# Folding a root-mean-square norm into the layer norm ahead of it, in a four-stage transformer kernel

## The reference, cut to what matters

```python
def _layernorm(x, axis=-1, eps=1e-05):
    m = mean(x); v = var(x)
    return (x - m) / sqrt(v + eps)

x = x + _L1_ffn_ref(_layernorm(x), ...)

def _L1_ffn_ref(hidden_states, norm_weight, router_w, ...):
    var = mean(square(hidden_states))                  # over the 128 features
    normed = hidden_states * rsqrt(var + 1e-08) * norm_weight
    probs = sigmoid(normed @ router_w.T)               # 8 experts, the best 2 are kept
    ...                                                # shared expert and 8 experts on normed
```

## Time and profile before

| | before |
|---|---|
| median of three runs | 5244.87 us |
| the profiled execution: its own time | 5246.2 us |
| the profiled execution: span of the trace | 5244.2 us |
| TensorE busy | 5028.0 us, 96% |
| VectorE busy | 3879.9 us, 74% |
| ScalarE busy | 3424.6 us, 65% |
| GpSimd busy | 2705.6 us, 52% |
| mean granted TensorE clock | 0.97 |

### The profile page before, as it was taken

The page is one execution under the profiler, slowest core; times in us unless marked ns, Lnnn a source line. Parts: engine busy times, 40 slices in busy tenths (PEclk is TensorE's granted clock), DMA queues, the critical chain, the costliest instruction groups (busy, mean ns, idle before and its releaser), DMA issues.

```text
span 5244.2 us, 175418 instructions
## 1 busy us (share of the span) xinstructions
PE 5028.0 (96%) x76384; PEld 3279.3 (63%) x76384; DVE 3879.9 (74%) x5095; ACT 3424.6 (65%) x5293; POOL 2705.6 (52%) x1425
## 2 busy tenths in 40 slices
PE   8899999999999999999999999986999999989999
PEld 5577777677777777777777777763333333266767
DVE  5888888888888888888888888846777677533333
ACT  2588888788888888888888877742666556621111
POOL 2877777777777777777777777731111111110000
PEclk8999999999999999999999999986999999979999
DMA  2011111111111111111111111103111111000000
GB/s 74 25 40 46 31 34 39 47 35 30 38 48 35 34 31 49 37 35 31 47 42 31 34 39 42 33 22 85 20 20 20 20 20 20 2 37 4 4 4 4
DMA packets 98013, 168.24 MB, mean 32 GB/s; under 512 B 25081, under 2 KB 36866, under 8 KB 96898
## 3 DMA queue, kind: packets, MB, share of 16 engines
q1 hardware_dynamic: 94402, 147.99, 10.4%
q10 hardware_dynamic: 2880, 9.44, 1.2%
HBM read 47.37 MB, written 10.49 MB: 11 GB/s over the span
## 4 chain that ended last, share of the span: by engine, by line
PE 32%; DVE 29%; issue 20%; ACT 16%; POOL 1%; SPq 1%; DMA 1%; ACTq 0%; DVEq 0%; POOLq 0%
DVE TOK L966 8%; DVE ss L857 8%; PE D L1414 5%; PE D L1436 5%; PE D L1123 5%; PE D L1517 5%; ACT L636 4%; DVE rs L906 4%; DVE mx L927 4%; PE D L1394 4%; ACT hh L636 4%; ACT kTb L623 3%; ACT kTb L627 1%; PE D L251 1%; DVE hh L947 1%
## 5 line engine op out<-in xcount | busy, mean ns | idle before, releaser
L473 POOL TENSOR_TENSOR rn<-ss,mhalf 128x33 f32<-128x33 f32 (+2 forms) x198 | 1095.7, 5534 | 332.9 <-DVE ss L859 315.7
L998 DVE TENSOR_REDUCE mxp<-D 128x2 f32<-128x1024 f32 (+3 forms) x640 | 675.6, 1064 | 239.6 <-PE D L1394 129.3
L477 POOL TENSOR_TENSOR hh<-hh,rr 128x1024 f32<-128x1024 f32 x192 | 365.4, 1903 | 469.2 <-DVE rr L911 469.2
L746 ACT ACTIVATE V<-D 128x1024 f32<-128x1024 f32 (+3 forms) x426 | 381.8, 897 | 245.3 <-PE D L1414 243.3
L966 DVE TENSOR_TENSOR TOK<-D,wA 128x1024 f32<-128x1024 f32 x384 | 466.5, 1215 | 0.0
L857 DVE TENSOR_REDUCE ss<-TOK 128x32 f32<-128x2048 f32 x192 | 437.1, 2276 | 0.0
L1330 PE MATMUL D<-PTb,V 64*64 64x32 f32 x24576 | 405.6, 220 | 6.0 <-issue 4.9
L1330 PEld LDWEIGHTS D<-PTb,V 64*64 64x64 f32 x24576 | 381.7, 135 | 32.0 <-issue 8.1
L906 DVE TENSOR_REDUCE rs<-hh 128x16 f32<-128x1024 f32 x192 | 234.2, 1220 | 205.9 <-ACT hh L636 205.9
L664 ACT ACTIVATE V<-D 128x512 f32<-128x512 f32 x384 | 229.7, 598 | 237.8 <-PE D L1298 173.0
L481 POOL TENSOR_TENSOR XC<-XC,TOK 128x1024 f32<-128x1024 f32 x128 | 303.1, 2368 | 47.7 <-DVE TOK L966 47.7
(11 more groups left out here) (240 smaller groups left out, 11877.1 us busy)
## 6 DMA issues: line engine op xcount, KB each, us to landing
V<-V SPq DMA_DIRECT2D x936, 64.0 KB, 2.0
V<-V SPq DMA_DIRECT2D x192, 192.0 KB, 2.5
RB<-watt_dram SPq DMA_DIRECT2D x12, 512.0 KB, 3.9
X<-watt_dram SPq DMA_DIRECT2D x12, 512.0 KB, 3.8
parts_dram<-hh SPq DMA_DIRECT2D x48, 128.0 KB, 2.4
TOK<-parts_dram ACTq DMA_DIRECT2D x36, 128.0 KB
RA<-parts_dram SPq DMA_DIRECT2D x12, 384.0 KB
X<-parts_dram SPq DMA_DIRECT2D x12, 384.0 KB
```

The costliest lines, as they stand in the source:

```text
L473: pool.tensor_tensor(rn[:, st % 2, lo:hi], ss[:, st % 2, lo:hi], mhalf[:, lo:hi], ALU.pow).then_inc(s["powed"], 1)
L477: pool.tensor_tensor(sh, sh, rr[:, :].unsqueeze(2).to_broadcast([P, HEADS, 64]), ALU.mult).then_inc(s["pnorm"], 1)
L746: act.activation(PTE[i % 3][:, 2 * hp:2 * hp + 2, 0:CH - r * P], pair_of(("S", i + LAG, hp))[:, :].rearrange("p (h n) -> p h n", h=2)[:, : ...
L998: dve.tensor_reduce(mxp[:, 2 * hp:2 * hp + 2, qt, kc], pair_of(("F", at, hp))[:, :].rearrange("p (h n) -> p h n", h=2)[:, :, 0:keys], AX.X ...
```

## The change

The second norm is no longer computed. The constant added to the mean square of the first norm becomes a multiplication and an addition, v * (1 + 1e-8) + 1e-5 * 1e-8, so that the power -0.5 of it is the factor of both norms. The applying instruction of this norm becomes a `scalar_tensor_tensor`, which multiplies the centred chunk by the norm's weight and by the spread factor and writes XS directly; so ScalarE's eight scalings go too. The load of `mvec` moves from the transfers of the experts' weights to ahead of the load of `wC`, with a semaphore of its own, `mvec_in`, for which VectorE waits ahead of the norm; `moew_in` counts six transfers. The other norms are computed as before.

```diff
         def norm_vector(dve, k, src, dst, after=None, rms=False):
...
                 if c >= 2:
                     dve.wait_ge(s["rstd_ready"], k * NC + c - 1)
-                dve.tensor_scalar(var_s[:, c % 2, :], PB[2 + c % 2][:, 0:NBLK], eps, None, ALU.add).then_inc(s["var_copied"], 1)
+                if rms:
+                    dve.tensor_scalar(var_s[:, c % 2, :], PB[2 + c % 2][:, 0:NBLK], 1.0 + EPS_RMS, EPS * EPS_RMS, ALU.mult, ALU.add)\
+                       .then_inc(s["var_copied"], 1)
+                else:
+                    dve.tensor_scalar(var_s[:, c % 2, :], PB[2 + c % 2][:, 0:NBLK], EPS, None, ALU.add).then_inc(s["var_copied"], 1)
...
+        def norm_apply(dve, k, c, dst, after, rms):
             dve.wait_ge(s["spread_ready"], k * NC + c + 1)
-            dve.tensor_tensor(dst(c), cen(c), PB[c % 2][:, :], ALU.mult).then_inc(s["normed"], 1)
+            if rms:
+                dve.scalar_tensor_tensor(chunk(XS, c), dst(c), mvec[:, 36:37], PB[c % 2][:, :], ALU.mult, ALU.mult)\
+                   .then_inc(s["normed"], 1)
+            else:
+                dve.tensor_tensor(dst(c), dst(c), PB[c % 2][:, :], ALU.mult).then_inc(s["normed"], 1)
...
# sync
                 straddling_windows(n)
+            sp.dma_start(mvec[:, :], t["mvec"]).then_inc(s["mvec_in"], 16)
             sp.dma_start(wC[:, :, :], t["wC"]).then_inc(s["w1att_in"], 16)
...
-            sp.dma_start(mvec[:, :], t["mvec"]).then_inc(s["moew_in"], 16)
...
# gpsimd
             norm_pool(pool, K_MOE)
-            norm_pool(pool, K_RMS)
...
# scalar
             norm_scalar(act, K_MOE, lambda c: chunk(XC, c))
-            norm_scalar(act, K_RMS, lambda c: chunk(XC, c), ready="normed")
-            act.wait_ge(s["moew_in"], 16 * 7)
-            for c in range(NC):
-                act.wait_ge(s["normed"], K_RMS * NC + c + 1)
-                act.activation(chunk(XS, c), chunk(XS, c), ACT.Copy, scale=mvec[:, 36:37]).then_inc(s["rms_scaled"], 1)
+            act.wait_ge(s["moew_in"], 16 * 6)
...
# vector
-            norm_vector(dve, K_MOE, lambda c: chunk(XR, c), lambda c: chunk(XC, c))
-            norm_vector(dve, K_RMS, lambda c: chunk(XC, c), lambda c: chunk(XS, c), center=False, eps=1e-8)
+            dve.wait_ge(s["mvec_in"], 16)
+            norm_vector(dve, K_MOE, lambda c: chunk(XR, c), lambda c: chunk(XC, c), rms=True)
...
# tensor
             norm_tensor(pe, K_MOE, lambda c: chunk(XR, c), "x3_ready", lambda c: c + 1)
-            norm_tensor(pe, K_RMS, lambda c: chunk(XC, c), "normed", lambda c: K_MOE * NC + c + 1, center=False)
...
-            pe.wait_ge(s["moew_in"], 16 * 7)
+            pe.wait_ge(s["moew_in"], 16 * 6)
             for c in range(NC):
-                pe.wait_ge(s["rms_scaled"], c + 1)
+                pe.wait_ge(s["normed"], K_MOE * NC + c + 1)
```

More of the change, by code:

```diff
@@ L31, in build_program @@
     EPS = 1e-5
+    EPS_RMS = 1e-8
     FF = 341
@@ L192, in build_program @@
             "oF_turned", "oF_copied", "out2", "x3_ready",
-            "moew_in", "rms_scaled", "xtok_turned", "xtok_copied", "logits", "probs", "rank_gt", "rank_eq", "rank_tri",
+            "moew_in", "mvec_in", "xtok_turned", "xtok_copied", "logits", "probs", "rank_gt", "rank_eq", "rank_tri",
             "rank_sum1", "rank_sum2", "rank", "chosen", "wsum", "winv", "comb",
@@ L237, in build_program, with norm_tensor @@
         block = ctx.enter_context(nc.Block())
-        def norm_tensor(pe, k, src, src_sem, src_at, center=True):
-            for c in range(NC if center else 0):
+        def norm_tensor(pe, k, src, src_sem, src_at):
+            for c in range(NC):
                 pe.wait_ge(s[src_sem], src_at(c))
@@ L262, in spread @@
                 pe.wait_ge(s["normed"], k * NC + c - 1)
-            elif k < K_RMS:
+            else:
                 pe.wait_ge(s["centered"], k * NC + NC - 1 + c)
@@ L267, in spread, with norm_vector @@
             m.then_inc(s["spread_ready"], 1)
-        def norm_vector(dve, k, src, dst, after=None, center=True, eps=EPS):
-            for c in range(NC if center else 0):
+        def norm_vector(dve, k, src, dst, after=None, rms=False):
+            for c in range(NC):
                 dve.wait_ge(s["mean_ready"], k * NC + c + 1)
@@ L276, in norm_vector, with norm_scalar @@
                     dve.wait_ge(s["rstd_ready"], k * NC + c - 1)
-                dve.tensor_scalar(var_s[:, c % 2, :], PB[2 + c % 2][:, 0:NBLK], eps, None, ALU.add).then_inc(s["var_copied"], 1)
+                if rms:
[3 more added lines that the diff above has]
+                    dve.tensor_scalar(var_s[:, c % 2, :], PB[2 + c % 2][:, 0:NBLK], EPS, None, ALU.add).then_inc(s["var_copied"], 1)
                 if c >= 1:
-                    norm_apply(dve, k, c - 1, src if not center else dst, dst, after)
-            norm_apply(dve, k, NC - 1, src if not center else dst, dst, after)
-        def norm_apply(dve, k, c, cen, dst, after):
+                    norm_apply(dve, k, c - 1, dst, after, rms)
+            norm_apply(dve, k, NC - 1, dst, after, rms)
+        def norm_apply(dve, k, c, dst, after, rms):
             dve.wait_ge(s["spread_ready"], k * NC + c + 1)
-            dve.tensor_tensor(dst(c), cen(c), PB[c % 2][:, :], ALU.mult).then_inc(s["normed"], 1)
+            if rms:
+                dve.scalar_tensor_tensor(chunk(XS, c), dst(c), mvec[:, 36:37], PB[c % 2][:, :], ALU.mult, ALU.mult)\
+                   .then_inc(s["normed"], 1)
+            else:
+                dve.tensor_tensor(dst(c), dst(c), PB[c % 2][:, :], ALU.mult).then_inc(s["normed"], 1)
             if after:
                 after(c)
-        def norm_scalar(act, k, dst, ready="centered"):
+        def norm_scalar(act, k, dst):
             for c in range(NC):
-                act.wait_ge(s[ready], (k if ready == "centered" else k - 1) * NC + c + 1)
+                act.wait_ge(s["centered"], k * NC + c + 1)
                 if c >= 2:
                     act.wait_ge(s["var_ready"], k * NC + c - 1)
-                elif ready == "normed":
-                    act.wait_ge(s["var_ready"], k * NC)
                 act.activation(SQ[:, c % 2, :], dst(c), ACT.Square).then_inc(s["squared"], 1)
@@ L317, in build_program @@
         K_MOE = K_ATT + 1
-        K_RMS = K_ATT + 2
         def ffn_of(st):
```

## The result

| | before | changed |
|---|---|---|
| median, runs taken with the changed kernel | 5247.61 us (6 runs) | 5224.92 us (6 runs, 5221.35 to 5233.88) |
| ratio, 95% interval | | 0.9957 [0.9947, 0.9967] |
| a second measurement on another occasion | 5246.46 us (15 runs) | 5231.71 us (11 runs), ratio 0.9972 [0.9963, 0.9981] |
| profiled execution: span | 5244.2 us | 5223.6 us |
| first mean matmul of the experts' norm to the loop | 78.90 us | 59.65 us |

The account below looks back on a forecast made before the run. TensorE's small matmuls and transposes were taken to bound the second norm. Terms 20.38 - 0 - 0 - 0 = 20.4 us, off the median 5244.87, gave 5224.5 us (0.83 within 2.5 us); range 5220.0 to 5229.5.

Parts of the forecast that it names:

- the 15 below which the prediction calls itself wrong: Stated failure test: wrong if the before-to-after difference is under 15 or over 26 us, or TensorE idles in the freed time.
- the clock's bounds: Times if the clock goes another way in transposes, router and first loop matmuls: 5219.6 to 5229.4 us; chance 0.10.
- What is removed: Second norm's stage on TensorE, from first norm's last spread to the residual's transposes: 20.38 us, all on the chain.
- One of the signs: Expected in the profile after: 128 fewer records of the one-column matmul line L251 and 8 fewer of L302.
- What is added: Longer applying instruction on VectorE, 0.06 us each, hidden behind TensorE: value 0, bounds 0 and +0.5 us.
- What is moved: Early mvec load ahead of wC, wanted 44 us later, and VectorE's new wait: cost 0, bounds 0 and 0.
- The clock: Clock's rises and falls in transposes and router move along unchanged: value 0, together about +4.9 and -4.9 us.
- The bound for a router wholly at the half clock: Router's 64 records all at the half clock: 13.6 us against 10.98, +2.7 us.
- the 0.5 allowed: Clock's effect on the loop's first 16 matmuls (8.43 us before): value 0, bounds +0.5 and -0.5 us.
- the sigmoid waits for the router's matmuls in both kernels: ScalarE's sigmoid behind the router: same wait before and after, so no cost counted.
- the jumps: Rival: the experts' loop's 7 jumps back need code reloads, giving 5240.6 or 5256.7 us; chance 0.04.
- The experts' weights: Rival: the removed stage covered their transfer or another engine; router waits, time stays near 5244.9 us; chance 0.03.

Follow-up runs that it names:

- e3: Changed kernel with TensorE's second-norm instructions put back, waiting for nothing and read by nobody; 5243.9 us, 1.0003 to before, stretch 79.54 us.
- e9: Kernel before with TensorE's second-norm work cut to one of four blocks per chunk, all waits kept; 5232.28 us (one run), stretch 70.75 us.
- e2: Changed kernel with the weight back on ScalarE: plain tensor_tensor application and eight scalings, second norm still gone; 5220.91 us (one run), stretch 58.48 us.
- e4: Kernel before with only the weight folded into the second norm's application and mvec loaded early; 5240.3 us, 1.0005, stretch 80.06 us.
- e7: Kernel before with the residual's transposes between the chunks of the second norm; 5239.31 us (one run), stretch 81.43 us.
- e8: Changed kernel without ScalarE's moew_in wait, residual's transposes moved behind the router and copied by ScalarE; 5223.17 us, 0.9957 to before, stretch 55.17 us.
- e10: Kernel before with the residual's transposes between the chunks of the first norm, second norm kept; 5241.95 us (one run), stretch 70.53 us.
- e6: Changed kernel without ScalarE's moew_in wait, residual's transposes between the norm's chunks; 5216.43 us, 0.9951 to before, stretch 49.00 us.

## Why the prediction was right

*The time:* 5224.5 was forecast and 5224.92 measured. A hit that close is luck. The difference of the medians is 22.7 us, not 20.4, and the reference's median had risen from 5244.87 us (3 runs) to 5247.61 (6 runs). The second measurement gives 14.7, just under the 15 below which the prediction calls itself wrong, with an interval of about 10 to 19 us. What bears the prediction out is the stretch, 19.25 us shorter, and not the medians. The three runs within 2.2 us, from which I had taken the scatter, misled me: 24 runs of the same kernel spread over 20 us, twice the width of the clock's bounds, and 0.83 for a time within 2.5 us was too much.

*What is removed:* 20.38 us was forecast and the chain shows just that stage gone. e3 (19.74 us of instructions that wait for nothing) and e9 (10.6 us with the same waits) show that it was TensorE's work, as the busy table had said, and not the round trip. (One of the signs was miscounted: 8 records a chunk are 64 and not 128, and the changed kernel has 64 matmul records fewer on that line, 320 instead of 384. L302 has 8 fewer, as said.)

*What is added:* the application takes 748 ns (751 taken, 687 before); behind the last one the gap to the first residual copy is 0.10 us (4643.91 to 4644.01), before 0.16. Value 0 was right. e2 carries it: no gain with the shorter instruction.

*What is moved:* it cost nothing. `wC` is issued at 3475.78 and its norm begins at 3514.20, 38 us later; it waits there for VectorE and not for the load. e4 shows no cost.

*The clock:* taken along with value 0 and right in the changed kernel for the transposes (6.03 us in both) and the router (10.70 and, in the second profile, 10.91, against 10.83). The bound for a router wholly at the half clock, 13.6 us, was met by e7, e8 and e10 at 13.47. The loop's first 16 matmuls took 7.90 us against 8.43 in the first profile, inside the 0.5 allowed, and 9.38 in the second, outside it: that bound was too narrow. As to the rule of the Trainium skill that I set against it ("TensorE: Matmul & The Clock Gate", Part 1, that the place of a rise varies from run to run): the two profiles of the changed kernel agree with it in the loop (7.90 and 9.38 us) and hardly differ in the router (10.70 and 10.91). Over all kernels with the transposes directly ahead of the router, the router took 10.55 to 11.74 us.

*What it missed:* the sentence "the sigmoid waits for the router's matmuls in both kernels", costed at nothing. Its table load, 1.28 us, was in ScalarE's timeline before, hidden behind the last scaling. The removal of the eight scalings put two waits next to each other, and the load came to stand between router and sigmoid. That is +1.2 us which the sum lacks: 19.2 instead of 20.4 in the stretch. It stayed inside the range, but it is the step that failed. I had asked of the removed scalings only whether anything waited for them, and not what had its place behind them.

*The rivals:* the loop takes 547.04 us before and 547.18 after, with 4 code packets of queue q8 before and 3 after in it, so the jumps did not become dear; the second round begins 68.9 us behind the first (4677.44 to 4746.30; 69.4 before). (The rule of the Trainium skill, "Runtime: NRT & Kernel Launch", Instruction fetch mechanics, that a taken branch to a target that is not at hand forces a fetch, is neither borne out nor contradicted: no run shows such a fetch.) The experts' weights were not late: TensorE has no wait ahead of the router.

## What to carry to other kernels

When a stage is removed, read what is left at the seams: on each engine, which waits become neighbours, and which once-only instruction (here a table load) had been hiding behind the removed work. Ask of a norm that works by one-column matmuls at what clock it runs: putting the residual's transposes between them, from a point where the clock is still full, was worth 9.2 us here (58.18 to 49.0), nearly half as much as removing a whole norm. From a point where it had fallen, the same edit cost 2.5 us (78.90 to 81.43). And when single runs scatter more than the effect, find a stretch in the profile that repeats, and time that.

## What the hardware showed that I had not expected

The same mix of work kept the full clock when entered at the full level (1.00 over 14.6 us, e6) and did not raise it when entered at the half level (0.50 over 26.5 us, e7), although TensorE had no idle time in the latter. Pure transposes did raise it: 2.1 us after their start in the changed kernel (granted clock 0.69 over 4644 to 4646), and the router's 10.55 to 11.74 us in every profile with transposes directly ahead of it, against 13.47 where it was entered at the half level without them (e7, e8, e10), says the same. What separates the two cases was not tested further.
